# Choosing the experts in slices beside the combining, in the last stage of a fused convolution and graph-gated mixture of experts

## The chip, the cores and the metric

One core of one Trainium2 chip runs the whole kernel as one program on five engines: TensorE (PE), VectorE (DVE), ScalarE (ACT), GpSimd (POOL) and SyncE (SP), which here only issues transfers. The metric is the device time in microseconds, the median of several runs. Less is better.

## The reference, cut to what matters

The input is 16 images of 64 channels and 56 x 56 pixels. A quantised convolution is added to it; then every pixel is a token (50176 of them) with 64 features. A graph attention over 262144 edges gives each token 16 numbers, `agg`. From these the experts are chosen:

```python
scores = _layernorm(agg, ln_gamma, ln_beta).reshape(M, HEADS, NUM_EXPERTS).mean(1)
topk_s, topk_i = jax.lax.top_k(scores, TOP_K)          # TOP_K = 2 of 4
w = jax.nn.softmax(topk_s, axis=-1)
out = jnp.zeros_like(x)
for ei in range(NUM_EXPERTS):
    g = jnp.where(topk_i == ei, w, 0.0).sum(-1)
    hh = jax.nn.gelu(x @ W1[ei] + b1[ei], approximate=False)
    out = out + g[..., None] * (hh @ W2[ei] + b2[ei])
return out
```

The result is `t + out`, written back as images.

## The kernel before, in words

The kernel is three programs, one after the other; between two of them all engines meet.

The first does the convolution and sorts the edges. The second works through groups of sorted edges: POOL gathers table rows, VectorE weighs them, TensorE scatters them by matmul, and VectorE adds them into `acc` (128 partitions x 392 columns x 20 values; a column `q` is 128 consecutive tokens). Beside that, the four experts' outputs of every token are computed and stored in `mlp_d`, and `x1_d` holds what they are added to. Both have long been complete when the edges are done.

At the end of the second program stands the choice of experts. VectorE works on all 392 columns at once: division by the sum of weights (L1432 to L1436), mean and centring (L1438 to L1442), scaling (L1446), sums over the heads (L1449), a rank for each expert by comparing each with each (L1462 to L1464), the exponential, and the gates `nb`. ScalarE helps with the square (L1189), the square root (L1191) and the exponential (L1193). Instructions of VectorE that depend on each other are chained by `L`, which waits for the semaphore of the instruction just issued. Each gate is then split into three bf16 parts (`parts`, L1479 to L1482). TensorE transposes them, 8 columns at a time (49 turns, L1303), VectorE copies each turn from PSUM to `gate_rows` (L1487), and SP stores it to `gate_d` (L1084).

The third program combines. Its unit is a chunk: 7 rows of pixels of an image's upper half and 7 of its lower half, 64 channels of each, so 392 elements on each of 128 partitions; there are 64 chunks, four to an image, eight to a pair of images. SP loads `mlp` (784 KB) and `X1` (196 KB) of six chunks ahead into eight buffers (L1516, L1517), loads a pair's gates from `gate_d` (L1523 to L1525), and stores each finished chunk as two halves (L1538). TensorE spreads the four gates of a chunk over the channels with four matmuls, into PSUM `A` or `C` (L1570). VectorE multiplies all four experts' outputs by them in one instruction (`gated`, L1603) and adds them in pairs (`pairs`, L1605). POOL adds the two pairs (`four`, L1584) and adds that to `X1` in place (L1586). `gated`, `pairs` and `four` have two buffers. A round of 16 chunks is written out, and the middle rounds are a hardware loop.

Of the kernel before, what the change touches and what calls it, by code (L numbers as in the profile page):

```python
# [15 lines left out]
P = 128  # L16
# [83 lines left out]
GQ = 8  # L100
GATE_BUFS = 8
PAIR_Q = 2 * HGT * WID // P

# [36 lines left out]
def build(nc, x, conv_w, conv_b, w_gat, att_src, att_dst, b_gat, ln_g, ln_b, w1, b1, w2, b2, edges, out):  # L140
    ctx = ExitStack()
    with ctx:
# [849 lines left out]

        with ExitStack() as ph:
            def tb(name, shape, dt=F32):
# [3 lines left out]
            acc = tb("acc", [P, NQ, VALS])  # L998
# [8 lines left out]
            na = tb("na", [P, NQ, HEADS])  # L1007
            nb = tb("nb", [P, NQ, HEADS])
# [7 lines left out]
            gate_rows = tb("gate_rows", [GQ * 3 * EXPERTS, GATE_BUFS, P], BF16)  # L1016
# [7 lines left out]
                "t_loaded0 t_loaded1 t_used0 t_used1 hidden gelu_ready expert_done expert_out "  # L1024
                "squares_ready sqvar_ready sqrt_ready exp_in exp_ready gates_split gates_turned gates_copied"
# [3 lines left out]
            gate_stored = [ctx.enter_context(nc.semaphore(f"gate_stored{k}")) for k in range(GATE_BUFS)]  # L1029
# [8 lines left out]

            parts = nodes[:].rearrange("p q f -> p (q f)")[:, 0:NQ * 3 * EXPERTS // 2].bitcast(BF16).rearrange("p (q e) -> p q e", e=3 * EXPERTS)
# [24 lines left out]
            def _(sp):  # L1064
# [16 lines left out]

                for k in range(NQ // GQ):
                    sp.wait_ge(s["gates_copied"], k + 1)
                    sp.dma_start(gate_d[k].rearrange("q e l -> (q e) l"), gate_rows[:, k % GATE_BUFS, :]).then_inc(gate_stored[k % GATE_BUFS], 16)  # L1084
                for k in range(GATE_BUFS):
                    sp.wait_ge(gate_stored[k], 16 * len(range(k, NQ // GQ, GATE_BUFS)))

# [13 lines left out]
            def _(act):  # L1101
# [86 lines left out]
                act.wait_ge(s["squares_ready"], 1)  # L1188
                act.activation(acc[:, :, 0:FEAT], nodes[:, :, 0:FEAT], ACT.Square).then_inc(s["sqvar_ready"], 1)  # L1189
                act.wait_ge(s["squares_ready"], 2)  # L1190
                act.activation(na[:, :, 1], na[:, :, 0], ACT.Sqrt, bias=eps_t[:], scale=1.0 / FEAT).then_inc(s["sqrt_ready"], 1)  # L1191
                act.wait_ge(s["exp_in"], 1)
                act.activation(nb[:], nb[:], ACT.Exp).then_inc(s["exp_ready"], 1)  # L1193

            @block.tensor
            def _(pe):
# [101 lines left out]
                for k in range(NQ // GQ):  # L1298
                    if k == 0:
                        pe.wait_ge(s["gates_split"], 1)  # L1300
                    if k >= 4:
                        pe.wait_ge(s["gates_copied"], k - 3)
                    pe.transpose(A[0:GQ * 3 * EXPERTS, k % 4, 0:P // 2].bitcast(BF16), parts[:, k * GQ:(k + 1) * GQ, :].rearrange("p q e -> p (q e)"), ident_h[:]).then_inc(s["gates_turned"], 1)  # L1303


            @block.vector
            def _(dve):
# [123 lines left out]
                agg, den = acc[:, :, 0:FEAT], acc[:, :, FEAT:VALS]  # L1431
                L(dve.tensor_scalar(na[:], den, 1e-16, None, ALU.add))  # L1432
                L(dve.reciprocal(nb[:], na[:]))
                dev = nodes[:, :, 0:FEAT]
                for h in range(HEADS):
                    L(dve.tensor_tensor(dev[:, :, h * DIM:(h + 1) * DIM], agg[:, :, h * DIM:(h + 1) * DIM],  # L1436
                                        nb[:, :, h:h + 1].broadcast_to([P, NQ, DIM]), ALU.mult))
                L(dve.tensor_tensor(dev, dev, over_nodes(vecs[:, 0, :], FEAT), ALU.add))  # L1438

                L(dve.tensor_reduce(na[:, :, 0], dev, AX.X, ALU.add))  # L1440
                L(dve.tensor_scalar(na[:, :, 1], na[:, :, 0], 1.0 / FEAT, None, ALU.mult))
                dve.tensor_tensor(dev, dev, na[:, :, 1:2].broadcast_to([P, NQ, FEAT]), ALU.subtract).then_inc(s["squares_ready"], 1)  # L1442

                scaled = lo_hot[:].rearrange("p b t l -> p (b t l)")[:, 0:NQ * FEAT].rearrange("p (q f) -> p q f", q=NQ)
                dve.wait_ge(s["squares_ready"], 1)
                L(dve.tensor_tensor(scaled, dev, over_nodes(vecs[:, 1, :], FEAT), ALU.mult))  # L1446
                dve.wait_ge(s["sqvar_ready"], 1)
                dve.tensor_reduce(na[:, :, 0], agg, AX.X, ALU.add).then_inc(s["squares_ready"], 1)
                L(dve.tensor_reduce(nb[:], scaled.rearrange("p q (h d) -> p q d h", h=HEADS), AX.X, ALU.add))  # L1449
                dve.wait_ge(s["sqrt_ready"], 1)  # L1450
                L(dve.reciprocal(na[:, :, 2], na[:, :, 1]))
                L(dve.tensor_tensor(nb[:], nb[:], na[:, :, 2:3].broadcast_to([P, NQ, EXPERTS]), ALU.mult))
                L(dve.tensor_reduce(amax[:], vecs[:, 2, :].rearrange("p (h d) -> p d h", h=HEADS), AX.X, ALU.add))
                L(dve.tensor_tensor(nb[:], nb[:], over_nodes(amax[:], EXPERTS), ALU.add))
                L(dve.tensor_scalar(na[:], nb[:], 1.0 / HEADS, None, ALU.mult))

                rank, beat = acc[:, :, 0:EXPERTS], acc[:, :, EXPERTS]
                for e in range(EXPERTS):
                    L(dve.memset(rank[:, :, e], float(EXPERTS - 1 - e)))
                for e in range(EXPERTS):  # L1460
                    for f in range(e + 1, EXPERTS):
                        L(dve.tensor_tensor(beat, na[:, :, e], na[:, :, f], ALU.is_ge))  # L1462
                        L(dve.tensor_tensor(rank[:, :, e], rank[:, :, e], beat, ALU.subtract))
                        L(dve.tensor_tensor(rank[:, :, f], rank[:, :, f], beat, ALU.add))  # L1464

                top, total = acc[:, :, EXPERTS], acc[:, :, EXPERTS + 1]
                L(dve.tensor_reduce(top, na[:], AX.X, ALU.max))
                dve.tensor_tensor(nb[:], na[:], acc[:, :, EXPERTS:EXPERTS + 1].broadcast_to([P, NQ, EXPERTS]), ALU.subtract).then_inc(s["exp_in"], 1)
                dve.wait_ge(s["exp_ready"], 1)
                L(dve.tensor_scalar(rank, rank, 1.5, None, ALU.is_lt))  # L1470
                L(dve.tensor_tensor(nb[:], nb[:], rank, ALU.mult))
                L(dve.tensor_reduce(total, nb[:], AX.X, ALU.add))
                L(dve.reciprocal(top, total))
                L(dve.tensor_tensor(nb[:], nb[:], acc[:, :, EXPERTS:EXPERTS + 1].broadcast_to([P, NQ, EXPERTS]), ALU.mult))

                for r in range(3):
                    part = parts[:, :, r * EXPERTS:(r + 1) * EXPERTS]
                    if r < 2:
# [4 lines left out]
                for k in range(NQ // GQ):  # L1483
                    dve.wait_ge(s["gates_turned"], k + 1)
                    if k >= GATE_BUFS:
                        dve.wait_ge(gate_stored[k % GATE_BUFS], 16 * (k // GATE_BUFS))
# [3 lines left out]
        with ExitStack() as ph:  # L1490
# [22 lines left out]
            def _(sp):  # L1513
# [15 lines left out]
                for k in range(AHEAD):  # L1529
                    load(k, k)  # L1530
# [103 lines left out]
```

## Time and profile before

| | us |
|---|---|
| median of 3 runs | 4511.31 |
| lowest and highest run | 4510.68 and 4512.57 |
| the profiled execution, its own time | 4502.82 |
| its span in the trace | 4501.1 |
| last addition into `acc` ends, choice begins | 4131.5 |
| last of `parts` written, first transpose | 4245.6 |
| first multiplication of the combining | 4278.3 |
| last addition of POOL ends | 4497.8 |

All times inside the kernel are those of the trace, counted from the start of its span. The time of an execution is slightly longer than its span, and the profiled execution is 8.5 us faster than the median of the runs. The first two programs, up to 4131.5 us, aren't touched by the change, apart from where some tiles lie.

### The profile page before, as it was taken

Reading aid. Unit: us, or ns where it says so; the run is one execution under the profiler, and the core shown is the slowest. Engines: PE = TensorE matmul, PEld = TensorE weight load, DVE = VectorE, ACT = ScalarE, POOL = GpSimd, SP = SyncE. Lnnn points to the kernel's source line nnn. Section 1 sums busy time; section 2 is a strip of 40 time slices with the busy share of each in tenths; the row PEclk is TensorE's granted clock in tenths of the full one; section 3 lists DMA queues with packets and bytes.
Section 4 is the critical chain, followed back from the end, with each engine's and each line's share of the span. In section 5 each row is a group of like instructions: output and inputs, shape, how many; then the busy total and the mean of one; then the engine's idle time right before and its main releaser. Section 6 shows DMA issues by size and latency. Waiting matters only on the chain. (4 is left out here: it accounts for less than half of the span.)

```text
span 4501.1 us, 61920 instructions
## 1 busy us (share of the span) xinstructions
PE 3514.0 (78%) x19005; PEld 2450.4 (54%) x19041; DVE 2830.1 (63%) x3531; ACT 1131.1 (25%) x2825; POOL 2904.8 (65%) x2928
## 2 busy tenths in 40 slices
PE   4686332588837999999999999999999999963143
PEld 1454232455525666666666666666666666663011
DVE  7778999888854454554554544545545545445788
ACT  0110000011103333334334333334343343320000
POOL 3000888787735777777777777777777777774055
PEclk8898555688866888989889888889898888876555
DMA  1243111599982222222222222222222222255099
GB/s 50 58 101 82 52 42 52 52 122 116 120 110 66 33 37 33 36 37 33 36 33 37 36 33 36 37 32 37 36 34 36 36 34 36 34 16 6 17 366 332
DMA packets 307960, 284.72 MB, mean 63 GB/s; under 512 B 203555, under 2 KB 280099, under 8 KB 307365
## 3 DMA queue, kind: packets, MB, share of 16 engines
q1 hardware_dynamic: 209556, 202.96, 20.8%
q0 software_dynamic: 87936, 29.35, 9.8%
q10 hardware_dynamic: 10384, 51.39, 5.3%
q8 instruction: 41, 0.67, 0.1%
q14 instruction: 43, 0.34, 0.0%
HBM read 161.21 MB, written 122.27 MB: 63 GB/s over the span
## 5 line engine op out<-in xcount | busy, mean ns | idle before, releaser
L1097 POOL DMA_INDIRECT gath<-tab_d,src_no x2192 | 2068.4, 944 | 752.7 <-issue 667.7
L463 POOL DMA_INDIRECT edge_d<-run_slots,slots x544 | 672.7, 1237 | 579.0 <-ACT run_slots L662 415.7
L1234 PEld LDWEIGHTS C<-spread,lo_hot 128*128 128x128 f32 x4384 | 804.7, 242 | 312.6 <-issue 215.9
L1234 PE MATMUL C<-spread,lo_hot 128*128 128x160 f32 x4384 | 875.9, 367 | 122.7 <-DVE spread L1394 119.5
L1406 DVE TENSOR_TENSOR acc<-acc,C 128x160 f32 x1096 | 351.7, 321 | 914.3 <-PE C L1234 773.1
L1220 PEld LDWEIGHTS C<-dst_rows,lo_hot_t 128*128 128x128 f32 x4384 | 558.6, 207 | 92.1 <-issue 78.3
L1220 PE MATMUL C<-dst_rows,lo_hot_t 128*128 128x32 f32 x4384 | 575.8, 288 | 12.2 <-ACT lo_hot_t L1115 12.2
L1129 ACT ACTIVATE mlp<-A,b2s 64x392 f32<-64x392 f32 x512 | 298.2, 582 | 943.7 <-PE A L1253 943.7
L1243 PE MATMUL A<-T,w1s 64*128 64x392 f32 x1024 | 530.3, 601 | 0.0
L575 PE MATMUL C<-wide_rec,hot_lo 128*128 128x136 f16 x2048 | 272.1, 305 | 299.1 <-DVE wide_rec L840 299.1
L1253 PE MATMUL A<-hid,w2s 128*64 128x392 f32 x1024 | 452.5, 524 | 0.0
L575 PEld LDWEIGHTS C<-wide_rec,hot_lo 128*128 128x128 f16 x2048 | 242.5, 123 | 352.6 <-DVE wide_rec L840 293.1
L1120 ACT ACTIVATE hid<-A,b1s 128x392 f32<-128x392 f32 x512 | 300.9, 588 | 473.8 <-PE A L1243 473.8
L1394 DVE TENSOR_TENSOR spread<-hi_hot,C 128x2560 f32<-128x2560 f32 x137 | 386.4, 2820 | 4.7
L1115 ACT COPY lo_hot_t<-A 128x512 f32<-128x512 f32 x548 | 293.1, 589 | 211.5 <-PE A L1210 211.5
L1210 PEld LDWEIGHTS A<-ident,lo_hot 128*128 128x128 f32 x2192 | 240.5, 142 | 187.4 <-issue 187.2
L1210 PE MATMUL A<-ident,lo_hot 128*128 128x128 f32 x2192 | 302.6, 282 | 36.2 <-PE A L1243 35.6
L1341 DVE TENSOR_TENSOR lo_hot<-C,lo 128x2048 f32<-128x2048 f32 x137 | 314.0, 2292 | 16.6
L1243 PEld LDWEIGHTS A<-T,w1s 64*128 64x128 f32 x1024 | 166.3, 203 | 245.6 <-issue 238.7
L1384 DVE TENSOR_TENSOR C<-gath,C 128x64 f32<-128x64 f32 x137 | 31.4, 229 | 420.8 <-DMA gath<-tab_d,src_no 416.3
L1584 POOL TENSOR_TENSOR four<-pairs 128x392 f32<-128x392 f32 x64 | 64.8, 1013 | 250.8 <-DVE pairs L1605 250.8
L662 ACT CAST run_slots<-C 128x136 f16<-128x136 f32 x32 | 10.0, 312 | 681.8 <-PE C L575 593.0
(268 smaller groups left out, 3266.4 us busy)
## 6 DMA issues: line engine op xcount, KB each, us to landing
mlp_d<-mlp ACTq DMA_DIRECT2D x128, 392.0 KB
mlp<-mlp_d SPq DMA_DIRECT2D x64, 784.0 KB, 6.0
gath<-tab_d,src_no POOLq DMA_INDIRECT x2192
pixels<-in_x SPq DMA_DIRECT2D x32, 392.0 KB, 8.5
src<-in_x SPq DMA_DIRECT2D x32, 392.0 KB, 9.3
T<-t_d SPq DMA_DIRECT2D x128, 98.0 KB
X<-x_d SPq DMA_DIRECT2D x64, 196.0 KB, 7.9
out<-X SPq DMA_DIRECT2D x128, 98.0 KB, 6.6
```

What stands on the lines that cost most here:

```text
L463: pool.indirect_dma_start(edge_d, bass.IndirectOffsetOnAxis(ap=slots[:, k, c:c + 1], axis=0), run_slots[:, k, c * RUN:(c + 1) * RUN, :].re ...
L575: mm = pe.matmul(C[:, k, 0:FIELDS * SLOT_COLS], hot_lo[:, j, t // LINE, :, t % LINE], fields[:, t // LINE, :, t % LINE], start=(j == 0 and ...
L1097: pool.indirect_dma_start(gath[:, g % BUFS, j, :], None, tab_d, bass.IndirectOffsetOnAxis(ap=src_no[:, t:t + 1], axis=0)).then_inc(gathere ...
L1120: act.activation(hid[:], A[:, 2, 0:CHUNK], ACT.Gelu, bias=b1s[:, e:e + 1]).then_inc(s["gelu_ready"], 1)
L1210: mm = pe.transpose(A[:, j // 4, (j % 4) * P:(j % 4 + 1) * P], lo_hot[:, k, half * G // 2 + j, :], ident[:])
L1220: mm = pe.matmul(C[:, 0, t * HI * HEADS:(t + 1) * HI * HEADS], lo_hot_t[:, t, :], dst_rows[:, k % 2, t // U].rearrange("p h f -> p (h f)") ...
L1234: mm = pe.matmul(C[:, bank, at:at + HI * VALS], lo_hot[:, k % UNROLL, u * U + j, :], spread[:, u * U + j].rearrange("p h v -> p (h v)"), s ...
L1243: pe.matmul(A[:, 2, 0:CHUNK], w1s[a, e, :], T[a, :], start=True, stop=True).then_inc(s["hidden"], 1)
L1253: pe.matmul(A[h * CH:(h + 1) * CH, 3, 0:CHUNK], w2s[:, e, :], hid[:], start=True, stop=True).then_inc(s["expert_done"], 1)
L1341: dve.tensor_tensor(lo_hot[:, k], lane_v.rearrange("p (k h) -> p k h", k=1).broadcast_to([P, G, P]), lo[:, bass.ds(g * G, G)].rearrange("p ...
L1394: dve.tensor_tensor(spread[:], hi_hot[:, k].rearrange("p t (h k) -> p t h k", k=1).broadcast_to([P, G, HI, VALS]), vals.rearrange("p t (k ...
L1406: L(dve.tensor_tensor(here, here, C[:, bank, at:at + HI * VALS].rearrange("p (h v) -> p h v", h=HI), ALU.add))
```

## The change

The choice leaves the second program. `acc`, `na` and `nb` stay allocated, and the third program has the choosing in it, in five slices of 1, 1, 2, 2 and 2 pairs of images (49 columns to a pair). `choose` is the same computation on a slice, in a somewhat different form: one division for all heads, sums over the heads by two additions, ranks by three shifted comparisons. Every engine that takes part follows the order of `in_turn`: the choice of slice k + 1 stands in front of the combining of slice k.

Turns have 7 columns in place of 8, 7 turns to a pair. They go through two PSUM buffers; ScalarE copies them and issues their stores, and ScalarE issues the loads of gates too. SP loads nine chunks at the start, into nine buffers, and reloads a buffer two chunks after its store was issued. The multiplication is done in two halves of two experts each, with three PSUM buffers for gates. POOL adds the pairs of three chunks of four, VectorE those of the fourth. All loops are written out.

```diff
-GQ = 8
+GQ = 7
+SLICES = ((0, 1), (1, 2), (2, 4), (4, 6), (6, 8))
+PAIR_TURNS = PAIR_Q // GQ
...
+            def pair_on_vector(n):
+
+                return n % 4 == 3
...
+            def in_turn(choose, combine):
+
+                choose(0)
+                for k in range(len(SLICES)):
+                    if k + 1 < len(SLICES):
+                        choose(k + 1)
+                    for p in range(*SLICES[k]):
+                        combine(p)
...
+                for n in range(NBUF):
+                    load(n)
+                for n in range(STEPS):
+                    k = n % NBUF
+                    sp.wait_ge(s["summed3"], n + 1)
+                    for h in range(2):
+                        sp.dma_start(out_rows[n // CHUNKS, n % CHUNKS, h], X1[h * CH:(h + 1) * CH, k]).then_inc(chunk_out[k], 16)
+                    if n >= LAG and n - LAG + NBUF < STEPS:
+                        sp.wait_ge(chunk_out[(n - LAG) % NBUF], 32 * ((n - LAG) // NBUF + 1))
+                        load(n - LAG + NBUF)
...
+                for k, (a, z) in enumerate(SLICES):
+                    q = slice(a * PAIR_Q, z * PAIR_Q)
+                    act.wait_ge(s["scaled_ready"], k + 1)
+                    act.activation(acc[:, q, 0:FEAT], acc[:, q, 0:FEAT], ACT.Square).then_inc(s["sqvar_ready"], 1)
+                    act.wait_ge(s["squares_ready"], k + 1)
+                    act.activation(na[:, q, 1], na[:, q, 0], ACT.Sqrt, bias=eps_t[:], scale=1.0 / FEAT).then_inc(s["sqrt_ready"], 1)
+                    act.wait_ge(s["exp_in"], k + 1)
+                    act.activation(nb[:, q], nb[:, q], ACT.Exp).then_inc(s["exp_ready"], 1)
+                    for i in range(a * PAIR_TURNS, z * PAIR_TURNS):
+                        act.wait_ge(s["gates_turned"], i + 1)
+                        if i >= GATE_BUFS:
+                            act.wait_ge(*stored(i - GATE_BUFS))
+                        act.copy(gate_rows[:, i % GATE_BUFS, :], turned_of[i % 2]).then_inc(s["gates_copied"], 1)
+                        act.wait_ge(s["gates_copied"], i + 1)
+                        act.dma_start(gate_d[i].rearrange("q e l -> (q e) l"), gate_rows[:, i % GATE_BUFS, :]).then_inc(gate_stored[i % GATE_BUFS], 16)
+                    for p in range(a, z):
+                        for i in range(p * PAIR_TURNS, (p + 1) * PAIR_TURNS):
+                            act.wait_ge(*stored(i))
+                        if p >= 2:
+                            act.wait_ge(s["gate_ready"], (p - 1) * PER * 2)
+                        load_gates(p)
...
+                def turn_gates(k):
+                    a, z = SLICES[k]
+                    pe.wait_ge(s["gates_split"], k + 1)
+                    for i in range(a * PAIR_TURNS, z * PAIR_TURNS):
+                        if i >= 2:
+                            pe.wait_ge(s["gates_copied"], i - 1)
+                        at = (i - a * PAIR_TURNS) * GQ
+                        pe.transpose(turned_of[i % 2], parts[:, at:at + GQ, :].rearrange("p q e -> p (q e)"), ident_h[:]).then_inc(s["gates_turned"], 1)
+
+                def spread_gates(p):
+                    pe.wait_ge(s[f"gate_loaded{p % 2}"], (p // 2 + 1) * 48)
+                    for n in range(p * PER, (p + 1) * PER):
+                        at = (n % PER) // CHUNKS * HGT * WID + n % CHUNKS * CHUNK
+                        for j in range(2):
+                            w = n * 2 + j
+                            if w >= 3:
+                                pe.wait_ge(s["gated_ready"], w - 2)
+                            for e in range(2):
+                                mm = pe.matmul(sums_of[w % 3][:, e], pick[:, 2 * j + e, :], gate_t[:, p % 2].rearrange("e q l -> e (q l)")[:, at:at + CHUNK],
+                                               start=True, stop=True)
+                            mm.then_inc(s["gate_ready"], 1)
+                in_turn(turn_gates, spread_gates)
...
+                for n in range(STEPS):
+                    if not pair_on_vector(n):
+                        pool.wait_ge(s["gated_ready"], n * 2 + 2)
+                        if n >= 2:
+                            pool.wait_ge(s["added"], n - 1)
+                        pool.tensor_tensor(pairs[:, n % 2], gated[:, n % 2, 0:2], gated[:, n % 2, 2:4], ALU.add).then_inc(s["paired_p"], 1)
+                    pool.wait_ge(*paired(n))
...
+                    L(dve.tensor_reduce(stat[:, :, 0], dev, AX.X, ALU.add))
+                    L(dve.tensor_scalar(stat[:, :, 1], stat[:, :, 0], 1.0 / FEAT, None, ALU.mult))
+                    L(dve.tensor_tensor(dev, dev, wide(stat[:, :, 1:2], FEAT), ALU.subtract))
+                    dve.tensor_tensor(mine, dev, over(vecs[:, 1, :], FEAT), ALU.mult).then_inc(s["scaled_ready"], 1)
+                    dve.wait_ge(s["scaled_ready"], k + 1)
+                    L(dve.tensor_tensor(mine[:, :, 0:8], mine[:, :, 0:8], mine[:, :, 8:16], ALU.add))
+                    L(dve.tensor_tensor(logit, mine[:, :, 0:4], mine[:, :, 4:8], ALU.add))
+                    dve.wait_ge(s["sqvar_ready"], k + 1)
+                    dve.tensor_reduce(stat[:, :, 0], dev, AX.X, ALU.add).then_inc(s["squares_ready"], 1)
+                    dve.wait_ge(s["sqrt_ready"], k + 1)
...
+                    for d in range(1, EXPERTS):
+                        m = EXPERTS - d
+                        L(dve.tensor_tensor(beat[:, :, 0:m], stat[:, :, 0:m], stat[:, :, d:EXPERTS], ALU.is_ge))
+                        L(dve.tensor_tensor(rank[:, :, 0:m], rank[:, :, 0:m], beat[:, :, 0:m], ALU.subtract))
+                        L(dve.tensor_tensor(rank[:, :, d:EXPERTS], rank[:, :, d:EXPERTS], beat[:, :, 0:m], ALU.add))
...
+                def combine(p):
+                    for n in range(p * PER, (p + 1) * PER):
+                        dve.wait_ge(chunk_in[n % NBUF], (n // NBUF + 1) * 32)
+                        if n >= 2:
+                            dve.wait_ge(*paired(n - 2))
+                        for j in range(2):
+                            w = n * 2 + j
+                            dve.wait_ge(s["gate_ready"], w + 1)
+                            dve.tensor_tensor(gated[:, n % 2, 2 * j:2 * j + 2], mlp[:, n % NBUF, 2 * j:2 * j + 2], sums_of[w % 3], ALU.mult).then_inc(s["gated_ready"], 1)
+                        if pair_on_vector(n):
+                            dve.wait_ge(s["gated_ready"], n * 2 + 2)
+                            dve.wait_ge(s["added"], n - 1)
+                            dve.tensor_tensor(pairs[:, n % 2], gated[:, n % 2, 0:2], gated[:, n % 2, 2:4], ALU.add).then_inc(s["paired_v"], 1)
+                in_turn(choose, combine)
```

## Rows read from the trace of the kernel before

**Rows 1.** Busy time of the engines over the span, from the page
```profile
PE 3514.0 (78%) x19005; PEld 2450.4 (54%) x19041; DVE 2830.1 (63%) x3531; ACT 1131.1 (25%) x2825; POOL 2904.8 (65%) x2928
```
**Rows 2.** Windows of the tail: busy us (instructions), granted clock, DMA share, GB/s
```profile
4131.40:4245.60 114.20, 0.00 (x1) 0.01 (x1) 108.71 (x52) 10.50 (x5) 0.00 (x0) 0.51 0.00 0
4245.60:4278.30 32.70, 16.39 (x56) 8.21 (x57) 10.17 (x49) 0.00 (x0) 0.00 (x0) 0.50 0.37 88
4278.30:4498.00 219.70, 92.49 (x250) 25.84 (x248) 189.21 (x128) 0.00 (x0) 129.51 (x128) 0.50 1.02 352
...
4300.00:4400.00 100.00, 43.55 (x118) 12.10 (x116) 85.35 (x59) 0.00 (x0) 59.00 (x59) 0.50 1.04 365
```
**Rows 3.** Groups of VectorE instructions of the choice, by shape
```profile
L1449 DVE TENSOR_REDUCE nb<-lo_hot 128x1568 f32<-128x6272 f32 x1 | 11.2, 11247 | 0.0
L1433 DVE RECIPROCAL nb<-na 128x1568 f32<-128x1568 f32 x1 | 10.0, 9952 | 0.0
L1436 DVE TENSOR_TENSOR nodes<-acc,nb 128x1568 f32<-128x1568 f32 x4 | 7.2, 1793 | 0.1
L1438 DVE TENSOR_TENSOR nodes<-nodes,vecs 128x6272 f32<-128x6272 f32 x1 | 6.7, 6692 | 0.0
L1464 DVE TENSOR_TENSOR acc<-acc 128x392 f32<-128x392 f32 x6 | 5.9, 976 | 0.2
L1432 DVE TENSOR_SCALAR na<-acc 128x1568 f32<-128x1568 f32 x1 | 1.0, 977 | 0.1
L1453 DVE TENSOR_REDUCE amax<-vecs 128x4 f32<-128x16 f32 x1 | 0.2, 178 | 0.0
```
**Rows 4.** Groups of instructions of the combining, by shape
```profile
L1605 DVE TENSOR_TENSOR pairs<-gated 128x784 f32<-128x784 f32 x64 | 77.2, 1206 | 2.2
L1603 DVE TENSOR_TENSOR gated<-mlp,A 128x1568 f32<-128x1568 f32 x32 | 57.0, 1783 | 26.1 <-DMA X<-x_d 25.7
```
**Rows 5.** Timeline around the square and the square root: start, duration
```profile
4170.62 5.43 ACT L1189 ACTIVATE acc<-nodes 128x6272 f32<-128x6272 f32 x1 [77.12 <-DVE nodes L1442]
4176.07 1.28 ACT L1191 ACT_TABLE_LOAD   x1
...
4183.98 0.99 ACT L1191 ACTIVATE na<-na,eps_t 128x392 f32<-128x392 f32 x1 [6.63 <-DVE na L1448]
```
**Rows 6.** Timeline of SP's queue, and a row of the DMA issues
```profile
4246.22 22.84 SPq L1084 DMA_DIRECT2D gate_d<-gate_rows  x49
...
4278.28 6.89 SPq L1524 DMA_DIRECT2D gate_t<-gate_d  x1
...
gate_d<-gate_rows SPq DMA_DIRECT2D x49, 24.0 KB, 1.5
```
**Rows 7.** Other ScalarE and POOL instructions, for their price
```profile
L662 ACT CAST run_slots<-C 128x136 f16<-128x136 f32 x32 | 10.0, 312 | 681.8 <-PE C L575 593.0 <-DMA edge_d<-run_slots,slots 88.8
...
L1133 ACTq DMA_DIRECT2D mlp_d<-mlp x128: 473/481/592, 1419.5 to 3957.2; - x128
...
L421 POOL MEMSET zero_row<- 128x512 f32 x1 | 0.5, 524 | 0.1
L404 POOL MEMSET ident<- 128x128 f32 x1 | 0.2, 204 | 0.0
```
**Rows 8.** Timeline of the combining: a first pairing, and the last instructions
```profile
4280.14 0.97 DVE L1605 TENSOR_TENSOR pairs<-gated 128x784 f32<-128x784 f32 x1
...
4494.16 1.38 DVE L1605 TENSOR_TENSOR pairs<-gated 128x784 f32<-128x784 f32 x1
4495.72 1.01 POOL L1584 TENSOR_TENSOR four<-pairs 128x392 f32<-128x392 f32 x1 [1.01 <-DVE pairs L1605]
4496.80 1.01 POOL L1586 TENSOR_TENSOR X<-X,four 128x392 f32<-128x392 f32 x1
```
**Rows 9.** A wait of the combining, and a transfer's KB and us to landing
```profile
DVE gated L1603 <- DMA X<-x_d: 34.2, 19, 11.6
...
out<-X SPq DMA_DIRECT2D x128, 98.0 KB, 6.6
```

More of the change, by code:

```diff
@@ L1429, in _ @@
                     body(TRIPS, k, True)
[L1431 to L1437, printed above, removed]
@@ L1445, in _ @@
[L1445 to L1451, printed above, removed]
@@ L1452, in _ @@
[L1452 to L1474, printed above, removed]
@@ new lines, in pair_on_vector, with paired @@
+            def pair_on_vector(n):
+                return n % 4 == 3
+            def paired(n):
+                mine = pair_on_vector(n)
+                return s["paired_v" if mine else "paired_p"], sum(pair_on_vector(m) == mine for m in range(n + 1))
+            def in_turn(choose, combine):
[5 more added lines that the diff above has]
+                        combine(p)
@@ L1520, in load_gates, with _ @@
+                for k in range(NBUF):
+                    sp.wait_ge(chunk_out[k], 32 * len(range(k, STEPS, NBUF)))
+            @block.scalar
+            def _(act):
+                def load_gates(p):
+                    half = p % 2
                     rows = gate_d.rearrange("k q e l -> e (k q) l")
                     low, high = gate_t[0:3 * EXPERTS, half], gate_t[3 * EXPERTS:2 * 3 * EXPERTS, half].rearrange("e q l -> e (q l)")
-                    first, whole = P - SHIFT_L, PAIR_Q - SHIFT_Q - 1
@@ L1523, in load_gates @@
-                    sp.dma_start(low, rows[:, bass.ds(pair * PAIR_Q, PAIR_Q), :]).then_inc(s[f"gate_loaded{half}"], 16)
-                    sp.dma_start(high[:, 0:first], rows[:, bass.ds(pair * PAIR_Q + SHIFT_Q, 1), SHIFT_L:P].rearrange("e q l -> e (q l)")).then_inc(s[f"gate_loaded{half}"], 16)
-                    sp.dma_start(high[:, first:first + whole * P].rearrange("e (q l) -> e q l", l=P),
-                                 rows[:, bass.ds(pair * PAIR_Q + SHIFT_Q + 1, whole), :]).then_inc(s[f"gate_loaded{half}"], 16)
@@ L1607, in _, with L @@
-                for t in range(STEPS):
-                    weigh_and_pair(0, t, True)
-                with dve.Fori(1, ROUNDS) as r:
-                    for t in range(STEPS):
-                        weigh_and_pair(r, t, False)
+                step = Signal(s["vstep3"])
+                def L(instr):
+                    link(dve, instr, step)
+                for e in range(EXPERTS):
+                    L(dve.memset(order[:, e:e + 1], float(EXPERTS - 1 - e)))
+                L(dve.tensor_reduce(beta[:], vecs[:, 2, :].rearrange("p (h d) -> p d h", h=HEADS), AX.X, ALU.add))
```

183 lines of the change are left out of this document (75 added, 108 removed).

## The prediction

> **What bounds the kernel now.** I read the page first, only to see where the changed work lies. Over the whole span TensorE is busiest [rows 1], but that says nothing here: the change touches only what follows the last addition into `acc`, at 4131.5 us of a span of 4501.1 us, so 369.6 us are at stake. I then cut that tail with the view of windows [rows 2]. It has three pieces. From 4131.4 to 4245.6 VectorE chooses experts (108.7 us busy of 114.2) and DMA share is 0.00: the choice is a serial VectorE program and the transfers stand still. From 4245.6 to 4278.3 the gates are transposed, stored, and loaded again. From 4278.3 to 4498 the 64 chunks are combined at a DMA share of 1.02. The groups of instructions of this piece [rows 4] give VectorE a need of 1.79 + 1.21 us a chunk; the actual pace is 219.7 / 64 = 3.43 us, and the chain of waits puts the difference down to loads of `X` (34.2 us in total) [rows 9]. So today's last piece is set by DMA and nearly by VectorE; POOL, with two additions of 1.01 us a chunk [rows 8], is well below both. The engines run one after the other, and the change wants them side by side. Whether it pays depends on what the new pace of a chunk is and on what still stands in line.
>
> **The cost of choosing.** All old operations have a duration that is nearly linear in elements per partition: 6272 elements take 6.69 us, 1568 take 1.79 us [rows 3], so a fixed 0.158 us and 1.04 ns an element; the 16 element row takes 0.178 us and confirms the fixed part. The next instruction of the linked chain starts some 0.03 us later, so an instruction costs 0.188 us before any element. Single operand forms take 0.98 us for 1568 elements, the reciprocal 6.2 ns an element, and operations whose neighbours lie apart 2.1 ns an element (0.976 us for 392) [rows 3].
> With these I priced the new `choose` at full width (392 columns) as if it were one slice of its 37 instructions:
> - the same as before: reciprocals of 1568 and twice 392 elements, 9.95 + 2.61 + 2.61, five operations of 6272 elements 33.5, the scalars, copies, and operations of 1568 elements as before;
> - the four divisions become one: 7.17 to 6.69 us;
> - the strided reduction (11.25 us [rows 3]) becomes additions of 3136 and 1568 elements, 3.43 + 1.79 us;
> - eighteen comparisons and rank updates (17.6 us) become nine over runs of 3, 2 and 1 columns. The rows have nothing like runs of 3; the bounds are 1.04 ns an element (8.8 us) and 2.1 ns (16.1 us). I take 10.0, since only the last run is of single columns;
> - the four fills become one copy, 0.98.
>
> Sum: 95.1 us, of which 37 x 0.188 = 7.0 fixed and 88.1 by elements. Five slices pay the fixed part five times: 88.1 + 35.0 = 123.1 us, against 114 before. A slice of one pair takes 18.0 us, of two 29.0.
> Each slice now waits for ScalarE. The square root's table load takes 1.28 us and starts when the square ends [rows 5]; VectorE meanwhile has one reduction of 0.98 us (1.79 in the wide slices), and the square root itself takes 0.3 to 0.4. That leaves about 0.6 us, five times: 3 us. The old code hid this under the 11.25 us reduction. The exponential's table load hides under six VectorE instructions in either size.
> In slice 1, ScalarE is also late with the square: its queue holds slice 0's seven turned copies with their stores (6.7 us, below), the wait for the last store (1.5 us to land [rows 6]) and three loads of gates. It is free some 10 us into the slice, VectorE asks after 7: 3 us more. Together 129.1 us of choosing. What VectorE runs while POOL still works off its backlog is slower: the pairing takes 0.97 us alone and 1.38 beside POOL [rows 8]. At 0.4 us for three or four instructions in each of three slices: 4.5 us.
>
> The Trainium skill (ScalarE: Activation LUTs, What ACT_TABLE_LOAD costs) speaks against this change: it gives a switch of table 1283 ns plus a drain of about 1380 ns. The trace agrees with the first number (1.28 us) and shows nothing that starts right behind a load; by that page the five waits would sum to some 8.5 us in place of 3, and the time would be 5 us longer.
>
> **What TensorE's order costs.** This is the wait that the change adds. In `in_turn`, TensorE's `turn_gates(k + 1)` stands in front of the spreading of the pair that VectorE wants next. Those transposes wait for `choose(k + 1)` and then go at the pace of ScalarE, because there are two buffers: copy, wait for one's own copy, issue the store. The copy is like that of 128x136 out of PSUM, 0.31 us, a store's issue on ScalarE's queue takes 0.48 us [rows 7]; with 0.16 us for the wait between, 0.95 us a turn. The old loop, with copies and issues on different engines, ran 49 turns in 22.84 us [rows 6], or 0.47 us each: that is the lower bound. TensorE sends its last transpose when all but two copies are done, so VectorE stands (turns - 2) x 0.95 + 1.4 us, where 1.4 is the first and last transposes and the first spread matmuls: 6.2 us before pair 0 (7 turns), 12.8 us after each of the three wide slices (14 turns): 44.6 us. By the lower bound it is 24.8.
> Behind TensorE nothing runs ahead: at most three half chunks of gates fit in PSUM and none has been spread for the next pair. After each such stall POOL waits another 2.0 us until two half products (0.975 us each, plus gaps) exist: 4 x 2.0 = 8.0 us.
>
> **The new pace.** VectorE now multiplies twice 0.975 us and pairs only each fourth chunk: 2.33 us a chunk. POOL gets the other three pairings, with 784 elements each. No POOL row has that form. Below, one call of 1.01 us (no dependence on size); above, two such calls, 2.02. POOL's fills take 0.524 us for 512 elements and 0.204 for 128 [rows 7], so a fixed part near 0.10, and POOL's additions scale: (1.01 - 0.10) x 2 + 0.10 = 1.92; with a fixed 0.18 it is 1.84. I take 1.88. POOL's successive instructions start 0.08 us after the end of the one before (4495.72 + 1.01 to 4496.80) [rows 8]. Four chunks are 3 x 1.88 + 8 x 1.01 + 11 x 0.08 = 14.6 us, 3.65 a chunk; 3.00 and 3.76 at the bounds. **POOL becomes the bound** of the combining, slower than today's 3.43. DMA needs 1.20 MB a chunk, 3.30 us at 365 GB/s (share 1.04 [rows 2]): just hidden. The ninth buffer and the loads issued in front cost nothing and bring only this: each run of chunks starts with nine in place. SP now waits for the output two chunks back, 7.3 us of POOL's time against 6.6 to land [rows 9]: hidden.
> 64 x 3.65 = 233.6 us. At the end of a run of pairs (8, 8 and 16 chunks) VectorE leaves for the next slice while POOL still has the last chunks: from the end of the pairing of the last but two, POOL has 8.5 us to go and VectorE 3.4, so 5.1 us overlap, three times: -15.3. That is all the overlap there is, since `gated` has two buffers.
>
> **Sum of the tail**, from 4131.5: change of program and five small instructions 2.0; choosing 129.1 + 4.5; TensorE's stalls 44.6; first products 8.0; POOL 233.6; overlap -15.3; last stores landing 3.3 (the last addition ends at 4497.8). Total 409.8 us against 369.6: **+40.2 us**. What is removed is in it: the 32.7 us of turning and loading of today's middle piece [rows 2]; the load of pair 0's gates now passes under `choose(1)`. The profiled execution took 4502.8 us with its span of 4501.1; the median of the runs is 4511.3. Added to the median: 4551.5 us.
>
> **Rivals.**
> *Less of a loss.* Turns at 0.47 us save 19.8 us: 4531.7. POOL's pairing at 1.01 us saves 64 x 0.65 = 41.6, of which DMA's 3.30 takes some 9 back, in the runs longer than nine chunks: 4519. For it: POOL spans are rough. Against it: a second operand and twice the elements, and POOL's own fills scale.
> *Faster.* POOL's additions might be held up today by VectorE's pairing, and run quicker once this is rarer, so that VectorE's 2.33 us sets the pace: 64 x 1.32 = 84 us less, 4467. It decides from a pace of (3.65 - 49.2 / 64) = 2.88 us downwards. Against it: with VectorE finished, the last two additions still take 1.01 us each [rows 8], and with these in eight of eleven places 3.00 is the floor. Only together with quick turns would the floor give 4499.
> *More of a loss.* The first slices run while nine chunks (9.0 MB, 25 us at 365 GB/s) are loading; today a load of gates that was issued behind six chunks held its queue for 6.89 us [rows 6]. If that happens on ScalarE, square and copies wait too: 7 us and, with stores landing in 6.6 instead of 1.5, 5 more in slice 1; again 4 to 7 us at the later loads of gates where VectorE is waiting: 4563 to 4580.
> *No effect.* The choice stays as long as it was and the pace stays DMA's: then the lost overlap equals the gain. It needs a pace of 3.65 - 40.2 / 64 = 3.02 us with turns at 0.95, close to the floor of 3.00.
>
> **Chances.** The forecast (POOL sets the pace, turns exposed; 4530 to 4572) 0.60. Less of a loss, 4503 to 4530: 0.20, of which 0.08 under 4520. Faster 0.10. More of a loss 0.10. A difference of 0.2% (9 us) is about what can be told from none: faster 0.10, same 0.08, slower 0.82. The range is 4512 to 4575, from a cheap pairing to the late queue.
>
> **What the next profile should show.** POOL's pairing near 1.88 us and POOL with idle of only 0.08 us inside a run of chunks, VectorE waiting there for POOL; a period of 14.6 us for four chunks. Three gaps of 12 to 13 us on VectorE between the last copy of `parts` and the next `gated`, filled by transposes at 0.95 us. Slices of 18 and 29 us plus waits. DMA share near 0 late in each wide `choose`, below 1 while combining. I am wrong if POOL's pairing is near 1 us, if four chunks take under 12 us, or if TensorE's gap is under 5 us.

## The result, and the profile after

The changed kernel takes 4541.96 us (median of 4 runs, 4539.83 to 4552.59) against 4511.0 us (4 runs): a ratio of 1.007, interval 1.0053 to 1.0087. The forecast was 4551.5, range 4512 to 4575, slower with 0.82. The profiled execution took 4539.83 us with a span of 4538.1.

The last addition into `acc` ends at 4138.2 us here, and the tail behind it takes 399.9 us. In the kernel before the tail was 369.8 us (the last addition ends at 4131.3 there), and 371.5 in a second profile of it (`e4_before`). The tail is what the rest of this text compares; as the two profiles of one kernel differ by 1.7 us, no difference of that size is read. The parts ahead of it, which the change doesn't touch, end anywhere from 4119.0 to 4140.5 us in the profiles of normal length below, so single spans compare badly.

Windows of the tail, the kernel after; they answer to [rows 2]: slices 0 and 1 with the first stall; eight chunks; slice 2 with its stall; and 120 us of the last run of chunks.
```profile
4138.30:4184.20 45.90, 5.04 (x17) 2.31 (x18) 34.66 (x79) 11.83 (x24) 0.00 (x0) 0.54 0.60 209
4184.20:4209.60 25.40, 11.84 (x30) 1.93 (x28) 16.59 (x18) 0.19 (x1) 22.57 (x18) 0.50 0.55 148
4209.60:4251.30 41.70, 5.33 (x18) 2.39 (x19) 30.29 (x39) 8.64 (x19) 7.24 (x5) 0.50 0.33 107
...
4410.00:4530.00 120.00, 54.50 (x135) 9.33 (x134) 66.90 (x72) 2.10 (x8) 108.74 (x84) 0.50 0.81 265
```
In the last run VectorE is busy for 67 us of 120, DMA at 0.81, POOL for 109: POOL sets the pace. The bound of the kernel before [rows 2], DMA at 1.02, is gone, and a slower one has come. In the third window POOL has 7 us of work in 42.

Groups of the tail of the kernel after, for [rows 3] and [rows 4]:
```profile
L1557 POOL TENSOR_TENSOR pairs<-gated 128x784 f32<-128x784 f32 x48 | 99.8, 2079 | 175.3 <-DVE gated L1642 175.3
L1642 DVE TENSOR_TENSOR gated<-mlp,A 128x784 f32<-128x784 f32 x86 | 80.9, 967 | 84.1 <-POOL pairs L1557 36.6 <-PE A L1545 24.2 <-issue 23.4
...
L1561 POOL TENSOR_TENSOR four<-pairs 128x392 f32<-128x392 f32 x64 | 64.9, 1014 | 3.8
L1646 DVE TENSOR_TENSOR pairs<-gated 128x784 f32<-128x784 f32 x16 | 16.6, 1040 | 0.5
L1513 ACT COPY gate_rows<-C 84x128 bf16<-84x128 bf16 x56 | 14.7, 262 | 64.9 <-PE C L1534 62.8 <-ACT gate_rows L1513 2.1
```
Of POOL's 175.3 us of idle time, the wait for VectorE's products, only the first 67 lie ahead of the first chunk (48 of them in the tail); the others are the three pauses of 36 us. VectorE waits for POOL inside the runs and for TensorE (24.2 us here, 10.0 with the other bank) behind the transposes. The time put down to "issue", 34 us with both banks, is a wait for POOL too: the one of 2.12 us that ends at 4423.02 ends as POOL's pairing does (4421.10 + 1.83). So VectorE waits 85 us for POOL in all.

Timeline of VectorE and POOL in the last run of chunks, kernel after (start, duration):
```profile
4421.10 1.83 POOL L1557 TENSOR_TENSOR pairs<-gated 128x784 f32<-128x784 f32 x1
...
4424.91 1.04 DVE L1646 TENSOR_TENSOR pairs<-gated 128x784 f32<-128x784 f32 x1
...
4425.07 2.57 POOL L1557 TENSOR_TENSOR pairs<-gated 128x784 f32<-128x784 f32 x1
...
4439.81 2.56 POOL L1557 TENSOR_TENSOR pairs<-gated 128x784 f32<-128x784 f32 x1
```
The same view behind the first eight chunks, where VectorE turns to slice 2:
```profile
4209.65 1.99 DVE L1588 TENSOR_SCALAR na<-acc 128x392 f32<-128x392 f32 x1
...
4211.67 2.60 DVE L1589 RECIPROCAL nb<-na 128x392 f32<-128x392 f32 x1
...
4214.31 1.90 DVE L1591 TENSOR_TENSOR acc<-acc,nb 128x1568 f32<-128x1568 f32 x1
4214.64 2.44 POOL L1564 TENSOR_TENSOR X<-X,four 128x392 f32<-128x392 f32 x1
4216.24 2.48 DVE L1592 TENSOR_TENSOR acc<-acc,vecs 128x1568 f32<-128x1568 f32 x1
```
The pairing takes 1.83 us when POOL is alone and 2.57 when it starts just behind VectorE's pairing. From one such row to the next, four chunks, it is 14.74 us: 3.69 a chunk. At 4214.64 and 4216.24 both engines stretch each other: 2.44 where 1.01 is usual, 2.48 where 1.79 is. The scalar instruction at 4209.65 takes 1.99 us where another of its size (L1606) takes 0.36.

Timeline of slice 2's turns, kernel after:
```profile
4241.22 0.36 DVE L1632 CAST parts<-nb 128x392 bf16<-128x392 f32 x1
...
4242.71 0.26 ACT L1513 COPY gate_rows<-C 84x128 bf16<-84x128 bf16 x1 [0.44 <-PE C L1534]
4243.00 0.32 ACTq L1515 DMA_DIRECT2D gate_d<-gate_rows  x1
...
4243.41 0.26 ACT L1513 COPY gate_rows<-C 84x128 bf16<-84x128 bf16 x1 [0.44 <-PE C L1534]
...
4251.29 0.97 DVE L1642 TENSOR_TENSOR gated<-mlp,A 128x784 f32<-128x784 f32 x1 [9.71 <-PE A L1545]
```
A turn (one transpose, its copy and its store) goes by in 0.70 us, and VectorE stands for 9.71.

### The profile page after: what moved, and what is told of

Read it like the earlier page. It is cut to its first block and busy times, and to the rows that moved or that the text cites. A ratio compares the mean times of both kernels' runs of the same rounds, so it can differ in the third digit from the quotient of the medians.

```text
span 4538.1 us, 61745 instructions
## 1 busy us (share of the span) xinstructions
PE 3550.3 (78%) x19012; PEld 2457.0 (54%) x19048; DVE 2783.5 (61%) x3636; ACT 1160.1 (26%) x2901; POOL 3021.5 (67%) x2976
## 5 line engine op out<-in xcount | busy, mean ns | idle before, releaser
L1225 PEld LDWEIGHTS C<-spread,lo_hot 128*128 128x128 f32 x4384 | 816.5, 245 | 299.8 <-issue 207.8
L1225 PE MATMUL C<-spread,lo_hot 128*128 128x160 f32 x4384 | 889.6, 371 | 103.8 <-DVE spread L1378 97.2
L1234 PE MATMUL A<-T,w1s 64*128 64x392 f32 x1024 | 540.0, 611 | 0.0
L1557 POOL TENSOR_TENSOR pairs<-gated 128x784 f32<-128x784 f32 x48 | 99.8, 2079 | 175.3 <-DVE gated L1642 175.3
```

What stands on the lines that cost most here:

```text
L1225: mm = pe.matmul(C[:, bank, at:at + HI * VALS], lo_hot[:, k % UNROLL, u * U + j, :], spread[:, u * U + j].rearrange("p h v -> p (h v)"), s ...
L1234: pe.matmul(A[:, 2, 0:CHUNK], w1s[a, e, :], T[a, :], start=True, stop=True).then_inc(s["hidden"], 1)
```

## The experiments

Three groups of four kernels ran on three chips. On the chip of the first group the second program, which no kernel changes, took some 2000 us longer (its last addition ended near 6100 us, and the kernel before took 6480.3 us there). The instructions of the tail had their usual durations, so for that group the tails are compared, not the totals. Tails are the span less the end of the last addition into `acc`.

| kernel | tail, us | VectorE busy in it | median, us | that group's before | ratio and interval |
|---|---|---|---|---|---|
| before, two profiles | 369.8, 371.5 | 308.1 | 4511.0 | | |
| after | 399.9 | 259.2 | 4541.96 | 4511.0 | 1.007 (1.0053 to 1.0087) |
| e1_half | 380.4 | 282.1 | 6496.15 | 6480.3 | 1.0019 (1.0000 to 1.0038) |
| e1_all | 361.3 | 308.2 | 6456.47 | 6480.3 | 0.9983 (0.9960 to 1.0007) |
| e2_turns | 365.0 | 259.2 | 6464.83 | 6480.3 | 0.9972 (0.9949 to 0.9994) |
| e3_inter | 409.9 | 303.0 | 6507.06 | 6480.3 | 1.0058 (1.0032 to 1.0084) |
| e4_six | 411.5 | 257.9 | 4540.68, one run | 4501.89 | |
| e4_form | 358.3 | | 4490.17 | 4501.89 | 0.9968 (0.9954 to 0.9981) |
| e4_best | 326.1 | 307.9 | 4463.07 | 4501.89 | 0.9907 (0.9888 to 0.9927) |
| e5_late | 399.9 | 260.0 | 4534.83, one run | 4499.1 | |
| e5_four | 317.4 | 301.6 | 4448.85 | 4499.1 | 0.9889 (0.9864 to 0.9913) |
| e5_eight | 351.8 | 328.3 | 4482.44, one run | 4499.1 | |
| e5_inter_all | 402.4 | 330.0 | 4532.48, one run | 4499.1 | |

**POOL's pace.** Two kernels move pairings from POOL to VectorE.
```diff
-                return n % 4 == 3
+                return n % 2 == 1        # e1_half; return True in e1_all
```


> Edit: VectorE pairs every second chunk in place of every fourth; the rest is the changed kernel, whose tail (last addition into acc to the end of the span) is 399.8 us. Theory (POOL's adding sets the pace of the combining): four chunks take 14.74 us now; without one pairing of 1.84 us but with a second delay of 0.73 us beside VectorE's pairing they take some 13.6, so the tail gets 15 to 25 us shorter, about 380. Rival A (the loads of chunks set the pace): the tail stays within 5 us. Rival B (VectorE's total work sets the end): VectorE has 16 pairings of 1.0 us more, so the tail gets some 16 us longer.

> Edit: VectorE pairs every chunk, POOL none. Theory (POOL's adding sets the pace): POOL then needs only 2.2 us a chunk and VectorE 2.9 to 3.2, near what the loads need (3.3); the pace falls from 3.69 us to 3.2 or 3.3, minus some overlap of POOL's backlog with the choosing: the tail is 15 to 30 us shorter than 399.8, VectorE no longer waits for POOL, and no POOL addition takes 2.57 us. Rival A (loads set the pace): within 5 us. Rival B (VectorE's total work): 48 pairings of 1.0 us more, 48 us longer.

e1_half: 19.5 us less; e1_all: 38.6 us less, more than was expected. VectorE's busy time grows by 23 and 49 us while the tail shrinks: its total work did not set the end of the changed kernel. Timeline of e1_all in its last run of chunks:
```profile
6378.03 1.01 POOL L1561 TENSOR_TENSOR four<-pairs 128x392 f32<-128x392 f32 x1 [0.91 <-DVE pairs L1647]
6379.13 1.01 POOL L1564 TENSOR_TENSOR X<-X,four 128x392 f32<-128x392 f32 x1
6381.05 1.01 POOL L1561 TENSOR_TENSOR four<-pairs 128x392 f32<-128x392 f32 x1 [0.91 <-DVE pairs L1647]
```
A chunk goes by each 3.02 us, with POOL waiting for VectorE in each. It is faster than the 3.30 us that I gave to the loads of a chunk at 365 GB/s, and VectorE never waits for a load: nine buffers that fill in each choice carry the run. In e1_half POOL has two pairings in four chunks, and VectorE's delay nearly all of them: 28 of POOL's 32 take 2.56 or 2.57 us, the other four, each the first of a run, 1.84.

**TensorE's order.** The transposes of the next slice go between the spreads of this one.
```diff
                             mm.then_inc(s["gate_ready"], 1)
+                        for _ in range(3):
+                            next(waiting, None)        # one transpose of turns(k + 1)
...
-                in_turn(turn_gates, spread_gates)
+                for _ in turns(0):
+                    pass
+                for k in range(len(SLICES)):
+                    waiting = turns(k + 1) if k + 1 < len(SLICES) else iter(())
+                    for p in range(*SLICES[k]):
+                        spread_gates(p, waiting)
```


> Edit: TensorE's transposes of slice k + 1 are put between the spreads of slice k, three behind each chunk, in place of ahead of all of them. Nothing else moves. Theory (VectorE and POOL stand behind the transposes, 9.7 us in each of three wide slices and 4.7 before pair 0): these gaps go, the tail falls by 30 to 34 us to some 367, about what the kernel before has (369.6). Rival (the stall is only moved: a spread behind three transposes at 0.7 us each comes too late for a chunk of 3.69 us, or the gates' load comes later and VectorE waits for it): the tail falls by less than 12 us.

The tail falls by 34.9 us. Waits of e2_turns in the tail (total us, times, longest) that answer to 24.2 and 10.0 us of the kernel after:
```profile
DVE gated L1651 <- PE A L1546: 1.7, 5, 0.6
DVE gated L1651 <- PE C L1546: 1.2, 3, 0.5
```
The wait is gone, not moved: it belonged to the order of the instructions alone. With this edit alone the changed kernel about equals the one before (365.0 against 369.8 and 371.5).

**Choosing between the chunks.** VectorE's `choose(k + 1)` is handed out in pieces, one piece behind each chunk of slice k, and TensorE transposes where that choice is complete.
```diff
-                in_turn(choose, combine)
+                for _ in choose(0):
+                    pass
+                for k, (a, z) in enumerate(SLICES):
+                    choosing = choose(k + 1) if k + 1 < len(SLICES) else iter(())
+                    for n in range(a * PER, z * PER):
+                        combine(n)
+                        for _ in range(-(-37 // ((z - a) * PER - 2))):
+                            next(choosing, None)       # one instruction of the choice
```


> Edit: VectorE's instructions of choose(k + 1) are issued between the chunks of slice k (some behind each chunk), and TensorE's transposes stand behind the chunk at which that choice is complete. POOL's and VectorE's shares of the pairing stay as in the changed kernel. Theory (the change loses because choosing and combining still take turns): now POOL works through the choosing, the tail falls from 399.8 to 300 to 330 us, with POOL busy nearly without a break. Rival (VectorE and POOL hold each other up when both read two tensors of SBUF, as POOL's 2.57 us in place of 1.84 beside VectorE's pairing): POOL's additions and VectorE's choosing stretch each other, and the tail stays above 350.

409.9 us, 10 more than the changed kernel: my theory fell, the rival held, but not alone. Groups of e3_inter in the tail:
```profile
L1610 DVE TENSOR_TENSOR scaled<-acc,vecs 128x1568 f32<-128x1568 f32 x3 | 8.4, 2797 | 0.1
L1568 POOL TENSOR_TENSOR four<-pairs 128x392 f32<-128x392 f32 x64 | 73.6, 1151 | 32.2 <-DVE pairs L1682 28.5
```
Waits of e3_inter in the tail:
```profile
POOL pairs L1564 <- DVE gated L1677: 182.5, 33, 95.0
...
DVE gated L1677 <- PE A L1546: 50.2, 6, 14.2
...
PEld A L1546 <- DMA gate_t<-gate_d: 37.0, 4, 10.5
```
VectorE's instructions are the same and take 43.8 us longer together (303.0 against 259.2); one of 1.79 us takes 2.80. POOL waits now inside the runs (33 times), since VectorE is the slower. And TensorE waits for gates to be loaded, 7 to 10 us each time: the choice of the next slice, behind which this load was hidden, no longer stands there. In VectorE's account the stretch costs 43.8 us and the waits for TensorE 32.7 more (66.9 against 34.2), while the waits for POOL shrink by 64 (from 85.5 to 21.5): that adds up to some 12, about the 10 us measured.

The same with `return True` for the pairings, so that POOL is busy 2.0 us a chunk:


> Edit on the kernel that issues the choosing between the chunks (tail 409.9 us): VectorE pairs every chunk there too, so POOL is busy 2.0 us a chunk in place of 3.6. Theory (that kernel lost because VectorE's two-tensor instructions wait for POOL, +43.8 us of VectorE's busy time, and because the load of gates is no longer hidden by a choice): with POOL half as busy VectorE is stretched by 10 to 25 us only, the waits for gates stay at some 40 to 60 us, and the tail is 365 to 395, still above the 326.0 us of the version that chooses between the slices. Rival (it was the interleaving's order of work, not the contention): the stretch stays above 40 us.

VectorE's busy time is 330.0 us, 22.1 more than e4_best's 307.9 with the same instructions, and it waits 56 us for spreads. Both were as expected, and the sum that I made of them wasn't: 326 + 22 + 56 is 404, where I wrote 365 to 395. It measures 402.4. So with POOL's work down from 3.6 to 2.0 us a chunk half of the stretch goes, which supports that the two engines hold each other up, and the wait for spreads, behind the exposed load of the gates, costs more than the stretch that is left.

**The loads.** Six buffers, and nine buffers with a late start:
```diff
-            NBUF = 9
+            NBUF = 6                                   # e4_six
```
```diff
+                sp.wait_ge(s["gates_split"], 2)        # e5_late
                 for n in range(NBUF):
                     load(n)
```


> Edit: six buffers for chunks in place of nine, so six chunks are loaded in front, and a buffer is loaded again four chunks ahead of its use. Theory (the transfers are hidden behind POOL's pace of 3.69 us; the early loading brings nothing that the kernel uses): the tail stays at 399.8 within 4 us. Rival (the early loads are what the change gains): the tail grows by 10 us or more and VectorE waits for X.

> Edit on the changed kernel: SP waits for the second slice's gates (gates_split 2) before its first load, so the nine chunks are loaded from some 41 us into the tail on, as late as they would be without the early loading; nine buffers stay. Theory (early loading brings only the first chunks; later the nine buffers fill in the next choice): the first multiplication comes 1 to 5 us later and the rest follows at POOL's pace, so the tail is 400 to 405 us against 399.8. Rival (the 12 us that six buffers cost came from the missing early loads, not from the short distance between load and use): the tail is 410 us or more.

Six buffers cost 11.6 us, three times my bound: this is a miss. The wait of VectorE in e4_six:
```profile
DVE gated L1642 <- DMA X<-x_d: 88.2, 42, 5.3
```
The late start of nine costs nothing (399.9), though VectorE then waits 8.3 us for the first chunks: 5.1 of them stand where TensorE's stall of 4.75 us stood, and the first product comes only 0.3 us later (46.3 us into the tail against 46.0). So the loading while the first slice is chosen is worth nothing in this kernel, where that stall and POOL's pace hide it; it wasn't tried in e4_best, which has neither. What counts is the number of buffers: with nine a buffer is loaded again seven chunks ahead of its use and not four, and nine chunks are in place at the start of a run and not six. No kernel parts these two. That VectorE's 42 waits go on to the end of the last run (the last one ends at 4529.44 of 4538.9 us) speaks for the distance.

**The parts by themselves.** The kernel before, with only the new form of the choice, at full width and in its old place:
```diff
-                L(dve.tensor_reduce(nb[:], scaled.rearrange("p q (h d) -> p q d h", h=HEADS), AX.X, ALU.add))
+                L(dve.tensor_tensor(scaled[:, :, 0:8], scaled[:, :, 0:8], scaled[:, :, 8:16], ALU.add))
+                L(dve.tensor_tensor(nb[:], scaled[:, :, 0:4], scaled[:, :, 4:8], ALU.add))
...
-                for e in range(EXPERTS):
-                    for f in range(e + 1, EXPERTS):
...
+                for d in range(1, EXPERTS):
+                    m = EXPERTS - d
```


> Edit on the kernel before, the choice left in its place and in one piece: sums over the heads by two additions in place of one strided reduction, ranks by three shifted comparisons in place of six single ones. Both theories count it the same way: 11.25 us become 5.2, and 17.6 become about 10, so the tail falls by 12 to 15 us from 369.7. It shows what the new form of the choice alone is worth, without the slices. Rival (the durations of these forms depend on more than their elements): less than 8 us.

13.2 us less of tail than in `e4_before`, on the same chip, and 11.7 in the medians. So 13 us of what the changed kernel gains come from the form of the choice and can be had without any slices. The kernel before, profiled again in that group:


> The kernel before, unchanged, profiled on the chip of this group, to have its tail (last addition into acc to the end of the span) beside those of the others. All theories: 369.7 us within 3, whatever the parts ahead of it take on this chip, because its durations come from VectorE and the transfers of the tail alone.

371.5 us; its first parts ended 3.5 us earlier than in the first profile.

**The versions that are faster.** e4_best has `return True` and TensorE's new order; e5_four has four slices in addition, e5_eight eight.
```diff
-SLICES = ((0, 1), (1, 2), (2, 4), (4, 6), (6, 8))
+SLICES = ((0, 2), (2, 4), (4, 6), (6, 8))              # e5_four
```


> Edit: both of the edits that helped alone, on the changed kernel: VectorE pairs every chunk, and TensorE's transposes stand between the spreads. Theory (POOL's pace cost 38.5 us of the tail and the stall behind the transposes 34.9, and they are independent): the tail is 399.8 - 38.5 - 34.9 = 326 to 332 us, 38 to 43 below the kernel before, whose total falls by about 40 us. Rival (below 350 the loads of chunks set the end, 3.3 us each at 365 GB/s): the tail stays at 340 or above and VectorE waits for X.

> Edit on the best version so far (VectorE pairs all chunks, transposes between the spreads, tail 326.0 us): four slices of two pairs in place of 1, 1, 2, 2, 2. Theory (VectorE is now the bound and each slice costs it 7.0 us of fixed parts and 0.6 us of waiting for the square root): one slice less, the tail is 7 to 9 us shorter, 317 to 319. Rival (the small first slices pay, since the combining starts earlier): the tail gets longer.

> Edit on the best version so far (tail 326.0 us): eight slices of one pair. Theory (7.6 us of VectorE for each slice more): three slices more, 23 us, the tail is 346 to 352. Rival (more, smaller slices overlap better): 330 or less.

e4_best's tail is 326.1 us: 38.6 and 34.9 us add up (399.9 - 73.5 = 326.4). It is 0.9907 of the kernel before. One slice less gives 8.7 us, three more cost 25.7, or 8.6 each. Window over the tail of e4_best:
```profile
4140.20:4466.60 326.40, 116.62 (x312) 24.51 (x312) 307.88 (x383) 38.24 (x81) 129.85 (x128) 0.51 0.72 247
```
The same of e5_four:
```profile
4118.70:4436.40 317.70, 117.88 (x312) 24.18 (x312) 301.55 (x346) 34.91 (x76) 129.64 (x128) 0.50 0.74 253
```
VectorE is busy for 94% and 95% of them. e5_four is the fastest, 4448.85 us, 0.9889 of its before (0.9864 to 0.9913), and what is left there is VectorE's own work. Against e4_form, which has the new choice and no slices (358.3 us), the third program with its slices is worth 32 us in e4_best and 41 in e5_four; how much of it is the overlap and how much the other order of turning, storing and loading wasn't measured.

## Why the prediction was right

The mechanism was right in both halves: POOL became the bound of the combining, and TensorE's order made VectorE and POOL stand behind the transposes. Each was taken away alone and gave 38.6 and 34.9 us, and both together 73.8. That the sum came within 10 us is in part luck, as errors of up to 7 us in it cancel. Sizes, term by term:

- *Choosing.* Foreseen 129.1 and 4.5 us. Slice 0 took 19.0, slice 1 21.2 (VectorE waits 2.2 us for the square, ScalarE being at the gates, where I had 3), the wide ones 31.9 each: 135.9. The 2.3 us over come from the stretch beside POOL, some 2.4 us in each wide slice where I had 1.5. Every added slice costs 8.6 us where the sum has 7.6.
- *Stalls of TensorE.* Foreseen 44.6, measured 34.2 (24.2 + 10.0). This is the term that was mis-sized. Its formula holds: with the measured turn, (turns - 2) x 0.70 + 1.4 is 4.9 and 9.8 us, for the measured 4.75 and 9.7 to 10.0. But the turn takes 0.70 us and not 0.95, mostly because the issue of a store takes 0.31 to 0.32 us on ScalarE's queue; the copy takes 0.26 in place of 0.31. I had taken the 0.48 us of [rows 7], from a transfer some nineteen times as large (392 KB against 21). That size is the reason is not shown: of the loads of gates, one of 147 KB is issued in 0.31 us and one of 2.2 KB in 0.49.
- *POOL.* Foreseen 3.65 us a chunk with a pairing of 1.88; measured 3.69 with 1.83, and 0.73 more for one pairing in each four chunks. The scaling by elements was right. Two errors nearly cancel, and that is luck: the delay beside VectorE's pairing, which I had read off for VectorE alone [rows 8], strikes POOL too, so the three pairings take 0.6 us more than foreseen; and the eleven gaps of 0.08 us, 0.88 in the sum, are 0.4 together.
- *First products.* Foreseen 8.0: 1.94 (4184.23 to 4186.17) each, 7.8.
- *Overlap.* Foreseen 5.1 us at each of three pauses; POOL ends 7.4 us after VectorE has turned away (4209.65 to 4217.08), its last addition stretched by VectorE's first instructions. That is 7.0 us more overlap over the three pauses, of which the stretched additions themselves eat 4.3 (1.43 each).
- *Sum.* 399.9 for a foreseen 409.8. Of the 9.9 us between, the stalls are 10.4. The rest cancels: choosing 2.3 more, POOL's runs 6.4 more (240.0 us, the stretched additions included), overlap 7.0 more, the first instructions 0.8 less.
- *The median* rose by 31 us, the tail by 28 to 30. The 37 us between the two profiled spans hold 7 of variation ahead of the tail.
- *The table load.* The Trainium skill's rule (ScalarE: Activation LUTs, What ACT_TABLE_LOAD costs) gives 1.38 us of drain behind a load. Here nothing of it is seen in front of the next activation:
```profile
4147.40 1.28 ACT L1506 ACT_TABLE_LOAD   x1
...
4148.69 0.38 ACT L1506 ACTIVATE na<-na,eps_t 128x49 f32<-128x49 f32 x1
```
The square root starts 0.01 us after the load's end, and VectorE waits 0.5 to 0.7 us a slice (2.9 in all), as summed from the rows; the 5 us on top don't exist.
- *What failed outright* was a side remark: that the buffers bring only what the first chunks need. Nine buffers in place of six (seven chunks of distance against four) are worth 11.6 us, loading early is worth nothing here. And 3.30 us a chunk was no floor: e1_all and e4_best go at 3.02 without a wait for a load, as the buffers fill while VectorE chooses.
- *The faster rival* said that POOL's additions might run quicker once VectorE pairs less. Where VectorE doesn't delay them they take 1.01 us in every version.
- *The rival of the late queue* did not come: with nine chunks loading, ScalarE issued its first loads of gates in 0.31 to 0.49 us. What it waited for ahead of them was its last store, 2.7 us to land (4163.60 to 4166.32) where I had 1.5.

Not settled: how much of the 43.8 us of stretch in e3_inter comes from POOL's reads and how much from its writes; no kernel parted them. It wasn't tried either whether a load of gates two slices ahead would let the interleaved kernel win.

## What to carry to other kernels

Before two stages are put beside each other, give every engine its time per unit of the joined loop: moving a share of the work to the engine that looked idle made that engine the bound, and undoing it gave 38.6 us. In an order that is shared by all engines, look for the one that has to finish a batch before it can serve the next unit; putting the batch between the units cost nothing and gave 34.9 us. Cutting a stage into slices has a price per slice (8.6 us here; in e5_eight 6.8 of it is VectorE's busy time for 37 more instructions, and the rest waiting), so slices pay only while there is something that they cover.

## What the runs showed that was not expected

- VectorE and POOL stretch each other when both work on tensors in SBUF, by some 0.6 to 1.6 us an instruction, and not in proportion to its length: POOL's pairing goes from 1.83 to 2.57 beside a VectorE pairing, its addition into `X` from 1.01 to 2.44; in e3_inter the most stretched VectorE instruction of 1568 elements (L1610) goes from 1.79 to 2.80 us on average, of 784 (L1613) from 0.97 to 1.96, of 392 (L1634) from 0.57 to 1.75. Short instructions suffer most for their length. Timeline of e3_inter:
```profile
6147.53 1.53 DVE L1634 TENSOR_TENSOR nb<-na,acc 128x196 f32<-128x196 f32 x1
6148.99 1.06 DVE L1636 COPY acc<-order 128x196 f32<-128x196 f32 x1
```
The same two take 0.36 and 0.26 us in slice 0, with POOL idle. The copy reads one tensor only. But not every instruction is stretched: in e3_inter the sums over a token's 16 values (L1604, L1618) never take more than the 1.79 us that they take alone, and the reciprocal at 4211.67 in the kernel after takes its 2.60 us with POOL at work beside it, whose additions keep their 1.01 us.
- The multiplication by gates out of PSUM isn't stretched: 0.967 us a half with POOL busy nearly always.
- The same second program took 2000 us longer on one of the chips, with TensorE's granted clock at 0.69 in place of 0.87 in one window of it (2000 to 2400 us). There POOL waited 1888 us for VectorE, which it doesn't elsewhere. Why isn't known.
